# Attention: the reciprocals of the softmax sums are spread over the heads' rows by a transfer on ScalarE's queue instead of VectorE's shuffle

## The reference, cut to what matters

```python
x = L0_attn_x                                  # (2, 512, 512), f32
x = x + attn(layernorm(x), w_q, w_k, w_v, w_o) # 32 heads of width 16
x = x + moe(layernorm(x), gate_w, w1, w2, w3)  # 8 experts, top 2, hidden 800
...
scores = jnp.einsum('bhqd,bhkd->bhqk', q, k) / jnp.sqrt(jnp.float32(D_K))
attn = jax.nn.softmax(scores, axis=-1)
out = jnp.einsum('bhqk,bhkd->bhqd', attn, v)
...
```

## Time and profile before

| what | us |
|---|---|
| three runs | 566.07, 573.68, 574.48; median 573.68 |
| span of the profiled execution, first to last instruction | 571.0 |
| TensorE busy | 550.3 (96%) |
| VectorE busy | 394.0 (69%) |
| ScalarE busy | 324.6 (57%) |
| GpSimd busy | 127.9 (22%) |

### The profile page before, as it was taken

How to read it: one execution, slowest core, us unless ns; L and a number is a source line. 1 busy time by engine, 2 the same in 40 slices (tenths; PEclk the granted TensorE clock), 3 DMA queues, 4 the chain that set the end, 5 groups by cost and what they waited for, 6 DMA issues and landing times.

```text
span 571.0 us, 9788 instructions
## 1 busy us (share of the span) xinstructions
PE 550.3 (96%) x3520; PEld 395.2 (69%) x3520; DVE 394.0 (69%) x730; ACT 324.6 (57%) x480; POOL 127.9 (22%) x153
## 2 busy tenths in 40 slices
PE   8999999999999999999998999999999999999991
PEld 6887664333333333333577988999999999999991
DVE  6915655699998999991588987673827466666650
ACT  4322114487778777778436463656646575657540
POOL 4300111001202212262301033234240321333112
PEclk9999997599999999999999999999999999999997
DMA  8290376906775575002283389695574758486122
GB/s 324 100 112 0 55 99 68 111 4 85 93 89 67 69 101 114 16 13 95 95 291 127 132 319 343 188 323 119 199 220 140 273 124 306 74 309 159 54 32 37
DMA packets 31116, 78.19 MB, mean 137 GB/s; under 512 B 9692, under 2 KB 10972, under 8 KB 26586
## 3 DMA queue, kind: packets, MB, share of 16 engines
q1 hardware_dynamic: 25770, 68.84, 46.0%
q0 software_dynamic: 5296, 8.69, 8.2%
HBM read 53.11 MB, written 9.32 MB: 109 GB/s over the span
## 4 chain that ended last, share of the span: by engine, by line
PE 78%; DVE 11%; DMA 4%; issue 2%; POOL 1%; ACT 1%; SPq 1%; POOLq 0%; DVEq 0%; ACTq 0%
PE ps L730 15%; PE ps L732 15%; PE ps L731 15%; PE ps_o L742 8%; DVE neg_max L1436 6%; PE ps L761 6%; PE ps L773 4%; PE ps_m L761 3%; DMA rec_row<-sum_rec 2%; DMA xn<-xn_rows,from_now 1%; PE ps L798 1%; PE ps_m L1013 1%; DVE rec_all L1511 1%; PE ps_o L779 1%; DVE stats L1406 1%
## 5 line engine op out<-in xcount | busy, mean ns | idle before, releaser
L1220 ACT ACTIVATE probs_t<-ps 128x1024 f32<-128x1024 f32 x128 | 124.3, 1022 | 39.3 <-PE ps L773 38.7
L1436 DVE TENSOR_REDUCE neg_max<-ps 128x1 f32<-128x512 f32 x170 | 111.3, 682 | 14.8 <-PE ps L761 12.2
L730 PE MATMUL ps<-xgT_hi,w_hi 128*128 128x256 f32 (+7 forms) x384 | 110.6, 288 | 0.9 <-DVE xgT_lo L1698 0.8
L731 PE MATMUL ps<-xgT_lo,w_hi 128*128 128x256 f32 (+7 forms) x384 | 109.7, 286 | 0.0
L732 PE MATMUL ps<-xgT_hi,w_lo 128*128 128x256 f32 (+7 forms) x384 | 109.7, 286 | 0.0
L761 PE MATMUL ps<-k_stack,q_stack 48*128 48x512 f32 x170 | 73.3, 479 | 1.6 <-issue 0.3
L730 PEld LDWEIGHTS ps<-xgT_hi,w_hi 128*128 128x128 f32 x384 | 72.7, 189 | 1.4 <-DVE xgT_lo L1698 0.9
L731 PEld LDWEIGHTS ps<-xgT_lo,w_hi 128*128 128x128 f32 x384 | 72.7, 189 | 0.1
L732 PEld LDWEIGHTS ps<-xgT_hi,w_lo 128*128 128x128 f32 x384 | 72.7, 189 | 0.0
L742 PE MATMUL ps_o<-probs_t,v_ones 128*32 128x512 f32 x512 | 70.8, 626 | 0.0
L773 PE MATMUL ps<-q_stack,k_stack 49*128 49x512 f32 x256 | 66.9, 448 | 0.4 <-ACT probs_t L1220 0.4
(11 more groups left out here) (328 smaller groups left out, 991.8 us busy)
## 6 DMA issues: line engine op xcount, KB each, us to landing
w_sb<-w SPq DMA_DIRECT2D x16, 1024.0 KB, 7.0
w_sb<-w SPq DMA_DIRECT2D x8, 1536.0 KB
w_sb<-w SPq DMA_DIRECT2D x8, 1152.0 KB, 8.0
q_stack<-q_hi SPq DMA_DIRECT2D x32, 128.0 KB, 5.4
k_stack<-k_hi SPq DMA_DIRECT2D x32, 128.0 KB, 5.0
q_stack<-q_lo SPq DMA_DIRECT2D x16, 128.0 KB, 4.5
k_stack<-k_lo SPq DMA_DIRECT2D x16, 128.0 KB, 6.2
q_hi<-o_norm SPq DMA_DIRECT2D x16, 128.0 KB, 4.4
```

The lines of the kernel that those rows point to most:

```text
L730: pe.matmul(o, x_hi, w_hi, start=start, stop=False)
L731: pe.matmul(o, x_hi, w_lo, start=False, stop=False)
L1220: a.activation(probs_t[:, kc % 2, 2 * half:2 * half + 2, :], ps4[:, 2 * (n % 2):2 * (n % 2) + 2, :], ACT.Exp, scale=D ** -0.5).then_inc(s_ ...
L1436: v.tensor_reduce(neg_max[:, g % 2, col:col + 1], max_bank(g, u2), AX.X, ALU.max, negate=True).then_inc(s_mx, 1)
```

## The change

SPREAD = 14: for groups 0 to 13 ScalarE issues one transfer for each group after the sixth exponential (u = 5) of step g + 2. It reads the four rows of rec_row, each 16 times, and writes the 64 even rows of rec_all, 2 KB each. It waits for rec_row's transfer (s_rb) and for the multiplication of the group before (s_on). GpSimd fills rec_all with ones once, so that the odd rows hold numbers, and waits for the transfer (s_wide) in place of the shuffle. Groups 14 and 15 keep the shuffle.

```diff
+SPREAD = NG - 2
+SPREAD_AT = 5
...
                     sp.wait_ge(s_rc, g + 1)
                     if g >= 1:
-                        sp.wait_ge(s_sh, g)
+                        sp.wait_ge(s_wide, 16 * min(g, SPREAD))
+                    if g > SPREAD:
+                        sp.wait_ge(s_sh, g - SPREAD)
                     sp.dma_start(rec_row[1:P:2 * D, :], sum_rec[:, g % 2, :]).then_inc(s_rb, 16)
...
             prepare(3)
+            pool.memset(rec_all[:, :], 1.0).then_inc(s_ones, 1)
 
             for g in range(NG - 1):
-                pool.wait_ge(s_sh, g + 1)
+                if g < SPREAD:
+                    pool.wait_ge(s_wide, 16 * (g + 1))
+                else:
+                    pool.wait_ge(s_sh, g - SPREAD + 1)
...
+                    if u == SPREAD_AT and 0 <= s - 2 < SPREAD:
+                        g = s - 2
+                        a.wait_ge(s_rb, 16 * (g + 1))
+                        if g == 0:
+                            a.wait_ge(s_ones, RING + 1)
+                        else:
+                            a.wait_ge(s_on, g)
+                        a.dma_start(rec_all[0:P:2, :],
+                                    rec_row[1:P:2 * D, :].unsqueeze(1).broadcast_to([GH, D, S])).then_inc(s_wide, 16)
...
-                    if u2 == 11 and g >= 0:
+                    if u2 == 11 and g >= SPREAD:
                         v.wait_ge(s_rb, 16 * (g + 1))
-                        if g >= 1:
-                            v.wait_ge(s_on, g)
+                        v.wait_ge(s_on, g)
                         v.stream_shuffle(rec_all[:, :], rec_row[:, :], [1] * 32).then_inc(s_sh, 1)
 
-            v.wait_ge(s_sh, NG)
+            v.wait_ge(s_sh, NG - SPREAD)
```

More of the change, by code:

```diff
@@ L260, in moe_layer @@
         s_sh = sem("s_sh")
+        s_wide = sem("s_wide")
         s_on = sem("s_on")
```

## The result

The changed kernel takes 595.4 us (median of 5, 592.6 to 605.2); the kernel before, measured again beside it, 566.5 us (median of 5, 565.1 to 574.5). The ratio is 1.053, 95% interval 1.050 to 1.056: slower by 28.9 us. Two of before's five executions and one of the changed kernel's ran some per cent longer at a lower clock, and the ratio leaves them out (565.1 to 566.5 against 592.6 to 599.3).

A forecast was written before the change was run, and what follows sets the result against it. TensorE was taken to carry 78% of the chain of waits, taking turns with VectorE in attention; 7.5 + 9.0 + 3.2 + 8.1 = +27.8 us on a median of 573.7 gave 601.5 us, range 582 to 634.

The forecast's parts named there:

- The loop: In attention, transfer to multiplication to next o_raw and back to the next transfer; free if shorter than 10.86 us.
- late end of attention: After step 14's o_raw, two transfers and multiplications delay the stores and the last shuffle by 2L - 0.5 = +8.1 us.
- L: Landing time of the new transfer from the start of its issue: 4.3 us alone, 6.5 us beside the stacks.
- Steps 2 to 6: Attention steps with stacks: a loop of L + 6.2 = 12.7 us against 11.2, +7.5 us in all.
- I take 4.8: In steps 2 to 6, 4.8 us from o_raw to the issue of the next transfer.
- Steps 7 to 9: Attention steps with stacks and max_rows a quarter later: a loop of L + 7.7 = 14.2 us, +9.0 us in all.
- the clock falls: Rival: new waits in attention bring TensorE back to 1.2 GHz, up to +73 us, 647 us; chance 0.12.
- Steps 10 to 13: Attention steps without stacks: a loop of 12.0 us with L = 4.3, +3.2 us in all.
- transfer-is-quick: Rival: the transfer spreads over 16 engines, L is 2.8 alone and 3.9 beside stacks; +7.3 us, 581 us; chance 0.13.
- all-is-hidden: Rival: no wait shows in attention and the 4.1 us gain stays, 569.6 us; chance 0.05.
- a shuffle is worth 0.34 us: In attention's busy loop a 0.74 us shuffle costs 0.34 us of time; 12 of them give at most 4.1 us.
- VectorE was to be off the chain: Sign: VectorE, at 11% of the chain of waits before, idles more and is no longer on it.

The follow-up runs named there:

- run 1: The change with SPREAD = NG - 4 in place of NG - 2, so groups 12 and 13 get their shuffles back; 589.1 us, ratio 1.036.
- run 10: Transfer only in groups 8 to 11, three kernels: as in the change; with a third o_raw buffer; with that and issue behind unit 7; 569.7, 573.0, 572.6 us.
- run 4: The change with rec_row sent ahead of max_rows and the transfer issued after u = 3 instead of u = 5; 588.4 us, ratio 1.038.
- run 5: The change with SPREAD = NG - 4 and a third o_raw buffer; 584.2 us, ratio 1.030.
- run 9: The change with SPREAD = NG - 4, a third o_raw buffer, issue behind unit 7 and two sets of source rows by group parity; 584.1 us, ratio 1.035.
- run 7: The kernel before, shuffle kept and no transfer, with only ScalarE's wait for rec_row added behind unit 5; 566.4 us, ratio 1.002.
- run 6: The kernel before, shuffle kept, plus the same transfer for groups 0 to 11 into a spare tile nobody reads; 580.8 us, ratio 1.028.
- run 8: The kernel before plus a same-shaped transfer from a constant tile into a tile nobody reads, without the wait for rec_row; 594.2 us, ratio 1.055.
- run 3: The change with neither shuffle nor transfer in groups 0 to 11, so results differ; only attention is compared, mostly 10.86 us a step; whole 603.8 us.

## Why the prediction was right, and where it wasn't

**The sum was right, its parts less so.** The loop and the late end of attention, which the prediction named, are there. But the terms of the table miss by -2.5, 0, +0.2 and -2.1, and a term that was not foreseen, +3.9, fills the gap: that the total is hit within 1.1 us is luck.

**The base.** 601.5 was forecast and 595.4 measured, 6.1 less. The forecast stood on the median of three runs, 573.7; five give 566.5, 7.2 less. The difference of the kernels was forecast as 27.8 us and is 28.9.

**L.** "I take 4.3" alone: 4.17 to 4.31. The reason was only half right. Four engines, yes (share 0.22). But "4 x 25 = 100 GB/s takes 1.3 us" was wrong, it is 48 GB/s and some 2.7 us. The lone transfer issued at 239.24, its GB/s in 40 bins from 239.2 to 243.5:

```profile
GB/s 29 25 1 0 0 0 0 0 0 0 0 57 57 76 38 38 57 38 57 57 38 57 38 57 57 38 38 76 38 38 76 38 38 57 38 19 0 0 0 0
```

Nor was the rest of L the 2.8 - 0.33 = 2.5 us of the store: 4.2 - 2.7 leaves 1.5. The two errors cancel, so 4.3 was luck. "I take 6.5" beside stacks: 6.0 to 6.8, and up to 8.0 in run 1.

**Steps 2 to 6, +7.5 predicted, +5.0 measured.** The loop is there, and its pieces add up: from o_raw at 143.02 to the issue at 147.23 it is 4.21, from there to the next o_raw at 154.65 7.42 = L + 1.4 with L = 6.0, together 11.63; the next one is 5.01 + 7.49 = 12.50. The first mis-sized term is "I take 4.8", which let the issue wait for the end of the exponentials of unit 5; it was made during them, and where rec_row had landed it came after 4.2. The second is L, 6.0 in these two steps in place of 6.5. Both sizes are those of one execution: in run 1, with the same code, these five steps were +9.1 us.

**Steps 7 to 9, +9.0 and +9.0,** by two errors that cancel. With the measured L of 6.0 to 6.1 the loop L + 7.7 gives 13.8, (13.8 - 11.2) x 3 = +7.8 for the three, and two steps took 13.60 and 13.64. The third took 15.01 at a granted clock of 0.77: the rival "the clock falls" was partly true beside my own case, not in place of it. It was priced for whole groups at half clock (up to +73) and came in three of the twelve steps, some 17 us at half clock, part of it hidden in the loop.

**Steps 10 to 13, +3.2 and +3.4,** and alone in run 10 the same: L + 7.7 with 4.2 is 11.9, measured 11.8 to 12.1.

**The end of attention, +8.1 and +6.0.** Both transfers stand on the path as forecast. From o_raw of step 14 the second store q_hi<-o_norm goes out 21.5 us on (290.23 - 268.74) where it was 15.4 (274.15 - 258.71). What was put too late is "the exponentials of u = 5 end at 264.4", 5.7 us behind o_raw: the issue is made during them, at 4.1 (272.86), which takes 1.6 of the 2.1 us off. Missed altogether is the gap behind attention, 3.7 us without work and 6 us at half clock, +3.9.

**What the prediction didn't have.** It named one wait as the price, so that removing it should give back the time. Runs 4, 5 and 9 removed it, and their medians lie 7 to 11 us under the change's; in the last two 6 of that belong to the end of attention (run 1), and against run 1 neither is clear of noise. The table shows the waits of the stretch of attention (us in total; the third column adds PEld's rows at ps and ps_m), the length of steps 2 to 13, and how long TensorE was at the 1.2 GHz level in them, worked out from each step's clock:

| kernel | o_raw for o_norm | ScalarE for rec_row | TensorE for max_rows | steps 2 to 13 | at 1.2 GHz | time |
|---|---|---|---|---|---|---|
| before | 0 | 0 | 2.0 | 133.4 | 0 | 566 |
| the wait alone (run 7) | 0 | 9.6 | 2.0 | 133.6 | 0 | 566.4 |
| the change | 21.3 | 9.9 | 2.4 | 150.8 | 17 | 595.4 |
| change, 12 groups (run 1) | 18.3 | 7.9 | 1.5 | 157.1 | 31 | 589.1 |
| earlier (run 4) | 2.0 | 12.0 | 8.9 | 146.8 | 20 | 588.4 |
| third buffer (run 5) | 0 | 19.2 | 6.2 | 150.3 | 38 | 584.2 |
| dead transfer (run 6) | 0 | 20.1 | 4.9 | 148.9 | 20 | 580.8 |
| third buffer, unit 7 (run 9) | 0 | 0 | 14.2 | 145.5 | 17 | 584.1 |
| dead transfer, no wait (run 8) | 0 | 0 | 16.6 | 160.3 | 38 | 594.2 |

Read downwards, the wait moves: from the loop to rec_row to the maxima's rows, and each arrangement with the transfer in 12 or 14 groups costs 15 to 29 us. What they have in common is 128 KB more in each step beside stacks that kept the DMA engines at a share of 0.44 to 0.69 in a step, and small transfers behind which ScalarE or TensorE stands. That the transfer makes these small ones late is shown (runs 6 and 8 against 7). How the engines divide their time between the two queues, and so why rec_row took 7.2 us in one step of run 6 and not in the others, isn't settled by these runs.

The last column but one is the second half of the price. Before and in run 7 TensorE never idles for more than 0.45 us at a time in these steps, and the clock stays at 1.00; each of the others has idle times of 0.7 us and more (5.0 at most), and behind some of them the 1.2 GHz level for 3 to 20 us. An estimate of its share: a step wholly at that level took 17.20 us (run 5, step 10), one without shuffle or wait 10.86, so a stretch at half clock loses about 0.37 of its length. That makes up to 14 of run 5's 17.0 us, 7 of run 6's 15.5, and at most 6 of the change's 17.4, of which the loop hides a part. So the third buffer did shorten the waits, and the fallen clock took most of it back. No run holds the clock and leaves the waits, so this split stays an estimate.

The transfer-is-quick and the all-is-hidden rivals fall: L was 4.2 to 6.8, and o_raw waited. That a shuffle is worth 0.34 us was right on the mean of eleven of the twelve steps (run 3); in all they are worth 3.7 us there, not 4.1. One sign failed: VectorE was to be off the chain, and it still has 5% of it.

## What to carry to other kernels

An instruction of 0.74 us on an engine that shares the bound may cost the time only 0.34; price that first, since it is all that a DMA in its place can win. Then ask of a new transfer not only who waits for its landing, but which small transfers are in flight beside it and who stands behind those: in a kernel whose DMA engines are busy for 0.44 to 0.69 of a step, 128 KB more a step moved the wait from place to place and never away. Taking away the wait that the profile names first gave back 5 of 24 us, not clear of noise. And read the granted clock step by step beside the waits: a step in which TensorE waits for nothing can be the longest of all (17.20 us at 0.51), for a stall of 1.14 us in the step before.

## What the runs showed of the hardware that was not expected

- A transfer out of four partitions ran at 48 GB/s from partitions 1, 33, 65, 97 and at 91 from 1, 37, 73, 109, on the same share of the engines (0.22 and 0.23). Beside the stacks the second landed later, in 7.1 to 8.3 us against 6.0 to 6.8 (5.8 to 8.0 in run 1, from the same partitions as the first).
- ScalarE issued the transfer during its own exponentials (issue at 147.23, the pair runs from 146.10 to 148.04), so where rec_row had landed the issue of 0.54 us was free; the prediction had put it behind them and charged about 0.6.
- Some of SyncE's issues of stacks, 0.6 us each before, took over 2 us beside the new queue:

```profile
135.97 2.12 SPq L480 DMA_DIRECT2D k_stack<-k_hi  x1
138.13 2.09 SPq L480 DMA_DIRECT2D q_stack<-q_hi  x1
```

- TensorE's clock: after 0.7 us (the change, at 131 us), 1.1 and 1.7 us (run 5), 2.3 us (run 10, third kernel) or 5.0 us (run 6) without work the granted clock fell to 0.50 and stayed there while TensorE was busy again: for 3 us in the change, 20 and 17 us in run 5, 7 us in run 10, 20 us in run 6. Not every such gap is followed by a fall: in the change none is behind 1.2 us at 167 us or 1.05 us at 194 us. A short stall is paid again in the work behind it, and the length of that is no measure of the stall.
